# A convolution, matching and cosine-transform kernel: 32-row matmuls widened, image 1 prepared later, norms from row sums, 42 unused matmuls

## The reference

```
x = x + attention(gn(x));   x = x + DCT2(gn(x))        # DCT along H and W, 48 x 48 matrices
attention, for each image:
  embed_w  = prelu(conv1x1(x, Wa));  raw_w = 6x6 patches of it, stride 2        # 576 patches
  match_in = prelu(conv1x1(x, W1));  xp    = 3x3 patches of it                  # 2304 queries
  ref      = prelu(conv1x1(mean over 2x2 of x, W2)); w = 3x3 patches of it      # 576 keys
  wn = w / max(sqrt(sum(w * w)), 1e-4)
  yi = softmax(10 * wn . xp, over the 576 keys)
  y  = transposed convolution of yi with raw_w (stride 2), then a 3x3 convolution Wd, stride 2, + bd, / 6
```

## Time and profile before

| | us |
|---|---|
| median of 3 runs (311.34 to 315.21) | 312.26 |
| the profiled execution, its own time | 313.37 |
| its span | 311.6 |
| TensorE busy in it | 255.3 (82%) |
| VectorE / ScalarE / GpSimd busy | 160.0 / 130.9 / 96.8 |
| chain that ended last, by engine | PE 62%, DVE 21%, issue 8%, ACT 7% |
| mean granted TensorE clock | 0.863 |

### The profile page before, as it was taken

One profiled execution on the slowest core, in us unless ns is written; L12 is line 12 of the kernel. 1 busy time (PEld: TensorE's weight loads), 2 busy tenths in 40 slices (PEclk: granted clock), 3 DMA queues, 4 the chain that ended last, 5 costly groups with the idle time before them and its releaser, 6 DMA issues.

```text
span 311.6 us, 4697 instructions
## 1 busy us (share of the span) xinstructions
PE 255.3 (82%) x1698; PEld 237.3 (76%) x1698; DVE 160.0 (51%) x343; ACT 130.9 (42%) x257; POOL 96.8 (31%) x98
## 2 busy tenths in 40 slices
PE   0458749966599999959989999999989899997085
PEld 0336748955588889949989899999978799996073
DVE  7544163247544363662266446467787664434722
ACT  2053035376346662442256846365646422121020
POOL 6220150077265343144041344339619200000000
PEclk9999999576555895985799999999999999999555
DMA  3430444000003004440000000000300000000321
GB/s 91 108 52 1 70 72 68 1 1 0 3 0 52 2 0 69 68 70 6 2 0 3 0 2 0 2 1 0 78 1 2 0 2 2 0 2 1 63 50 38
DMA packets 11494, 7.67 MB, mean 25 GB/s; under 512 B 8496, under 2 KB 10608, under 8 KB 11344
## 3 DMA queue, kind: packets, MB, share of 16 engines
q1 hardware_dynamic: 11168, 6.94, 12.3%
q10 hardware_dynamic: 304, 0.45, 0.4%
HBM read 2.14 MB, written 1.18 MB: 11 GB/s over the span
## 4 chain that ended last, share of the span: by engine, by line
PE 62%; DVE 21%; issue 8%; ACT 7%; POOL 1%; DVEq 0%; ACTq 0%; POOLq 0%
PE zt L730 21%; PE ps L710 8%; PE yt L745 8%; PE pm L662 6%; PE pm L622 4%; DVE negm L1174 3%; PE pm L684 3%; PE pm L777 3%; DVE yl L1189 3%; PE pd L757 2%; DVE bnst L993 2%; ACT nt L899 2%; DVE v L1212 2%; PE zt L710 2%; PE pm L693 2%
## 5 line engine op out<-in xcount | busy, mean ns | idle before, releaser
L730 PE MATMUL zt<-ident,nt 128*125 128x128 f32 (+1 forms) x720 | 94.8, 284 | 0.0
L730 PEld LDWEIGHTS zt<-ident,nt 128*125 128x125 f32 (+1 forms) x720 | 90.8, 186 | 1.1 <-issue 0.2
L526 POOL TENSOR_TENSOR nt<-nt 128x599 f32<-128x599 f32 (+1 forms) x42 | 56.2, 1338 | 46.9 <-ACT nt L907 39.7
L1189 DVE TENSOR_TENSOR yl<-zt,yh 125x384 fp32r<-125x384 f32 (+1 forms) x60 | 33.4, 556 | 46.6 <-ACT yh L915 15.3
L915 ACT ACTIVATE yh<-zt 125x384 fp32r<-125x384 f32 (+1 forms) x60 | 29.2, 487 | 46.9 <-PE zt L730 46.8
L899 ACT ACTIVATE nt<-ps,negm 128x576 f32<-128x576 f32 x32 | 23.8, 745 | 47.5 <-DVE negm L1174 47.5
L907 ACT ACTIVATE nt<-nt,rps 128x599 f32<-128x599 f32 x36 | 28.7, 798 | 11.8 <-DVE rps L1181 11.5
L516 POOL TENSOR_TENSOR ml<-vim,mh 128x384 fp32r<-128x384 f32 x12 | 12.3, 1029 | 65.3 <-ACT mh L871 65.2
L745 PE MATMUL yt<-yh,kh 125*128 125x384 f32 (+1 forms) x60 | 24.7, 411 | 7.1 <-DVE yl L1189 7.0
L1212 DVE SCALAR_TENSOR_TENSOR v<-pd,v 32x384 f32<-32x384 f32 (+3 forms) x48 | 26.2, 547 | 4.1 <-PE pd L757 2.7
L1174 DVE TENSOR_REDUCE negm<-ps 128x1 f32<-128x576 f32 x32 | 24.1, 753 | 7.6 <-PE ps L710 7.5
(11 more groups left out here) (160 smaller groups left out, 433.1 us busy)
## 6 DMA issues: line engine op xcount, KB each, us to landing
vim<-mimg SPq DMA_DIRECT2D x24, 72.0 KB, 2.5
v<-mimg SPq DMA_DIRECT2D x36, 24.0 KB, 1.9
v<-x SPq DMA_DIRECT2D x2, 288.0 KB, 4.0
vim<-mimg SPq DMA_DIRECT2D x12, 48.0 KB, 2.2
x_copy<-v SPq DMA_DIRECT2D x2, 288.0 KB, 3.1
xr<-x_copy SPq DMA_DIRECT2D x4, 144.0 KB, 2.9
out<-res SPq DMA_DIRECT2D x8, 72.0 KB, 2.2
x<-x SPq DMA_DIRECT2D x6, 72.0 KB, 2.0
```

Source lines behind the costliest of these rows:

```text
L526: pool.tensor_tensor(nt[:, dst, (to + 1) * KP + 1:(to + 1) * KP + 1 + n], nt[:, one, (row1 + 1) * KP + 1:(row1 + 1) * KP + 1 + n], nt[:, o ...
L730: last = nc.tensor.matmul(turned(zt[:, m % 2, :], n, dh, col, JW), keys_at(tile, r + dr, n, shift), ident[:, :], start=at == 0, stop=at == ...
L1189: nc.vector.tensor_tensor(yl[0:n, blk, :].rearrange("p (h j) -> p h j", j=W), turned(zt[:, m % 2, :], n), F(yh[0:n, blk, :]).rearrange("p ...
```

## The change

- The convolutions take no 32-row matmuls. `conv2` and, for image 0, `conv1` use all 128 rows of `x4` in full precision, against weights that are zero outside one quarter (`wb2`, `wb1`, made by one scaling with a mask `smask`). The embedding, and `conv1` of image 1, use a stack of 96 rows `x3`: reduced x, the rest, reduced x again, against stacked weights `wsta`, `wst1`, so that one matmul does the work of three. `x3` is loaded by three DMAs of x per image (`load_copies`).
- The norm adds the squares of three rows on GpSimd first (`sv`), and takes 6 matmuls where it took 18.
- Ahead of the loop the chores have four banks (`bank`), two of them lent by `yt` and `pd`. Keys are scaled and split in halves. The ninth taps of block 0 are loaded from ScalarE's queue.
- The zeroing of the tile edges, of `mr` and of `wr` moves to ScalarE.
- Image 1's x, with one buffer for both images now, is loaded after conv1 of image 0, and its jobs stand in other gaps.
- `warm`: 16, 8, 6 and 12 matmuls of ones with ones into a bank that nobody reads.

The core of the diff:

```
 BEFORE = [
-    ("xs", (0,)), ("mean", (0,)), ("weights", (0,)), ("bias", (0, 1)), ("conv2", (0, 1)), ("low", (0,)),
+    ("xs", (0,)), ("warm", (0,)), ("mean", (0,)), ("weights", (0,)), ("warm", (1,)), ("bias_2", (0,)), ("conv2", (0, 1)), ("bias_1", (0,)),
     ("conv1", (0, 1)), ("squares", (0,)), ("conv1", (2, 3, 4, 5, 6, 7)), ("norm", (0,)),
-    ("inorm", (0, 1)), ("keys", (0,)), ("split", (0, 1)), ("bias", (2,))]
+    ("warm", (2,)), ("inorm", (0, 1)), ("ninth", (0,)), ("xh", (0, 1)), ("keys", (0, 1)), ("split", (0, 1)), ("warm", (3,))]
+
+WARM = (16, 8, 6, 12)
...
 SPREAD = [
-    ("emb", 0, 2, 4, 2), ("ek", 0, 2, 9, 2), ("xs", 1, 1, 13, 1), ("mean", 1, 1, 15, 1), ("weights", 1, 1, 19, 1),
-    ("bias", 1, 3, 22, 1), ("residual", 0, 1, 28, 1), ("conv2", 1, 2, 26, 1), ("low", 1, 1, 27, 1),
-    ("conv1", 1, 8, 29, 1), ("squares", 1, 1, 31, 1), ("norm", 1, 1, 37, 1), ("inorm", 1, 2, 40, 1),
-    ("keys", 1, 1, 42, 1), ("emb", 1, 2, 46, 2), ("ek", 1, 2, 51, 2), ("residual", 1, 1, 60, 1),
+    ("wst", 0, 1, 1, 1), ("xl", 0, 2, 1, 1), ("bias_a", 0, 1, 3, 1), ("emb", 0, 2, 6, 3), ("ek", 0, 2, 12, 2),
+    ("xs", 1, 1, 16, 1), ("mean", 1, 1, 19, 1), ("xh", 1, 2, 20, 1), ("xl", 1, 2, 22, 1), ("weights", 1, 1, 22, 1),
+    ("bias_2", 1, 1, 24, 1), ("wst", 1, 1, 25, 1), ("bias_1", 1, 1, 26, 1), ("conv2", 1, 2, 26, 1), ("bias_a", 1, 1, 28, 1),
+    ("residual", 0, 1, 28, 1), ("conv1", 1, 8, 30, 1), ("squares", 1, 1, 30, 1), ("norm", 1, 1, 35, 1),
+    ("inorm", 1, 2, 39, 1), ("keys", 1, 2, 42, 1), ("emb", 1, 2, 47, 2), ("ek", 1, 2, 52, 2), ("residual", 1, 1, 60, 1),
...
+        def bank(n):
+
+            if n < nbefore:
+                return (pm[:, 0, :], pm[:, 1, :], yt[:, :], pd[:, :])[n % 4]
+            return pm[:, n % 2, :]
...
             def load_x(b, quarters):
                 src = x[b].rearrange("c h w -> c (h w)")
+                if b:
+                    sp.wait_ge(s_mf, misc_no["conv1", b - 1, ROWS - 1] + 1)
...
+            def load_copies(b):
+
+                if b:
+                    sp.wait_ge(s_xl[b - 1], 2)
+                for k in range(3):
+                    sp.dma_start(x3f[C * k:C * (k + 1), :],
+                                 x[b].rearrange("c h w -> c (h w)")).then_inc(s_x3[b], 16)
...
             load_x(0, range(2))
             output_weights()
-            load_x(1, range(4))
+            load_copies(0)
             for b in range(B):
                 sp.dma_start(x1(b), x[b].rearrange("c h w -> c (h w)")).then_inc(s_xin[b], 16)
             sp.dma_start(cosm[:, :], dct).then_inc(s_cos, 16)
             ref_patches(0)
+            load_x(1, range(4))
             match_patches(0)
+            load_copies(1)
             ref_patches(1)
             match_patches(1)
...
-                pool.memset(nt[:, :, 0:KP], 0.0).then_inc(s_tiles, 1)
-                pool.memset(nt[:, :, PT - KP - 2:], 0.0).then_inc(s_tiles, 1)
-                pool.memset(strided(nt[:, 0, :], KP, (PT, NTILES), (KP, HL)), 0.0).then_inc(s_tiles, 1)
...
+                pool.wait_ge(s_sq[b], 2)
+                link(pool.tensor_tensor(sv[:, :], sq[:, 1:1 + L], sq[:, 1 + WL:1 + WL + L], ALU.add))
+                pool.tensor_tensor(sv[:, :], sv[:, :], sq[:, 1 + 2 * WL:1 + 2 * WL + L], ALU.add).then_inc(s_sv[b], 1)
+                pool.wait_ge(s_sv[b], 1)
...
                 n = misc_no[name, b, i]
-                if n >= 2:
-                    wait_emptied(pe, *plan[n - 2])
-                return pm[:, n % 2, :]
+                if n < nbefore:
+                    if n >= 4:
+                        wait_emptied(pe, *plan[n - 4])
+                else:
+                    wait_emptied(pe, *plan[max(n - 2, nbefore - 1)])
+                return bank(n)
...
-                for n, (w, v) in enumerate(((wsh, xh), (wsh, xl), (wsl, xh))):
-                    last = nc.tensor.matmul(o, w[rows, at:at + width], v, start=n == 0, stop=n == 2)
...
-                    last = conv(o[0:96, REFQ * k:REFQ * (k + 1)], q, S_W2, 96, x2h[rows, :], x2l[rows, :])
+                    last = nc.tensor.matmul(o[0:96, REFQ * k:REFQ * (k + 1)], wb2[:, 2 * i + k, :], x2[:, :],
+                                            start=True, stop=True)
...
             def conv1(b, i):
-                if i == 0:
-                    pe.wait_ge(s_wst[b], 1)
-                    pe.wait_ge(s_x4l[b], 1)
+
                 o = misc("conv1", b, i)
-                q, cols = i // 2, slice(HALF * (i % 2), HALF * (i % 2 + 1))
-                rows = slice(C * q, C * (q + 1))
-                conv(o[0:96, 0:HALF], q, S_W1, 96, x4h[rows, cols], x4l[rows, cols]).then_inc(s_mf, 1)
+                if b == 0:
+                    pe.wait_ge(s_wb1, 1)
+                    pe.wait_ge(s_x4[b], 16 * 4)
+                    last = nc.tensor.matmul(o[0:96, 0:HALF], wb1[:, i // 2, :],
+                                            x4[b][:, HALF * (i % 2):HALF * (i % 2 + 1)], start=True, stop=True)
+                else:
+                    pe.wait_ge(s_wst[b], 2)
+                    pe.wait_ge(s_xl[b], i // 4 + 1)
+                    last = nc.tensor.matmul(o[0:96, 0:HALF], wst1[:, :], x3[:, HALF * i:HALF * (i + 1)], start=True,
+                                            stop=True)
+                last.then_inc(s_mf, 1)
...
+                v = x3[:, HALFQ * i:HALFQ * (i + 1)].rearrange("p (i u j v) -> p i u j v", u=2, j=WL, v=2)
+                for n in range(4):
+                    at = C * (3 - n)
+                    last = nc.tensor.matmul(o[:, 0:HALF], wsta[:, at:at + 128], v[:, :, n // 2, :, n % 2],
+                                            start=n == 0, stop=n == 3)
...
-                    for r in range(3):
-                        at = WL * r + 96 * n + 1
-                        last = nc.tensor.matmul(o[0:96, n:n + 1], sq[:, at:at + 96], ones[0:96, 0:1], start=r == 0,
-                                                stop=r == 2)
+                    last = nc.tensor.matmul(o[0:96, n:n + 1], sv[:, 96 * n:96 * (n + 1)], ones[0:96, 0:1], start=True,
...
+            def warm(_, i):
+
+                pe.wait_ge(s_const, 2)
+                for _ in range(WARM[i]):
+                    nc.tensor.matmul(zt[:, 0, 0:128], ones[:, :], ones[:, :], start=True, stop=True)
...
+            def zeros():
+
+                act.wait_ge(s_const, 2)
+
+                def zero(dst, done):
+
+                    shape = list(dst.shape)
+                    one = strided(ones[0:shape[0], :], 0, *[(0, n) for n in shape[1:]])
+                    nc.scalar.activation(dst, one, ACT.Copy, scale=0.0).then_inc(done, 1)
+
+                zero(nt[:, :, 0:KP], s_tiles)
+                zero(nt[:, :, PT - KP - 2:], s_tiles)
+                zero(strided(nt[:, 0, :], KP, (PT, NTILES), (KP, HL)), s_tiles)
+                zero(mr[:, :, :], s_zero)
+                for b in range(B):
+                    zero(wr[b][:, :], s_zero)
...
+            def x3_high(b, i):
+
+                act.wait_ge(s_x3[b], 48)
                 if b:
                     act.wait_ge(s_mf, misc_no["emb", b - 1, 1] + 1)
-                nc.scalar.activation(x4h[:, :], x4[b][:, :], ACT.Copy).then_inc(s_x4h[b], 1)
-                act.wait_ge(s_x2[b], 1)
-                nc.scalar.activation(x2h[:, :], x2[:, :], ACT.Copy, scale=0.25).then_inc(s_x2h[b], 1)
+                cols = slice(HALFQ * i, HALFQ * (i + 1))
+                nc.scalar.activation(x3[:, cols], x3f[:, cols], ACT.Copy).then_inc(s_xh[b], 1)
...
+                for n in range(3):
+                    nc.scalar.dma_start(v2[CR * n:CR * (n + 1), 0:CHUNK],
+                                        mimg[64:64 + CR, at:at + CHUNK]).then_inc(s_mim[0], 16)
...
+            def x3_low(b, i):
+
+                dve.wait_ge(s_xh[b], i + 1)
+                part, cols = slice(C, 2 * C), slice(HALFQ * i, HALFQ * (i + 1))
+                nc.vector.tensor_tensor(x3[part, cols], x3f[part, cols], F(x3[part, cols]),
+                                        ALU.subtract).then_inc(s_xl[b], 1)
...
+                nc.vector.scalar_tensor_tensor(out=wb2[:, :, :], in0=strided(par[:, :], P_W2, (0, 4), (1, 96)), scalar=root,
+                                               in1=strided(smask[:, :, :], 4, (1, 4), (0, 96)), op0=ALU.mult,
+                                               op1=ALU.mult).then_inc(s_wb2[b], 1)
...
+                mid = slice(3 * C, 4 * C)
+                link(nc.vector.tensor_copy(wsta[:, mid], wsf[:, F_WA:F_WA + C]))
+                nc.vector.tensor_tensor(wsta[64:96, mid], wsf[64:96, F_WA:F_WA + C], F(wsta[64:96, mid]),
+                                        ALU.subtract).then_inc(s_wst[b], 1)
...
+            def keys_low(b, i):
+
+                wait_emptied(dve, "inorm", b, i)
+                dve.wait_ge(s_wsc[b], i + 1)
+                dve.wait_ge(s_whi[b], 2 * (i + 1))
+                cols = slice(HALF * i, HALF * (i + 1))
```

(21 more changed lines are left out.)

228 lines of the change are left out of this document (104 added, 124 removed).

## The result

The changed kernel took 277.83 us (median of 277.30 to 278.40), the kernel before beside it 313.05: ratio 0.887, 95% interval 0.881 to 0.893, 11.3% faster. The forecast was 265, in a range of 252 to 285. The profiled execution took 277.30, its span 275.5.

A forecast was written before the change was run, and what follows sets the result against it. The prediction took a chain through all engines to bound the first stage, and TensorE, often at the low clock, the rest. Gains of 14.5, 12.8 and 20.9, together 48.2 us, gave 265 us, in a range of 252 to 285.

The forecast's parts named there:

- First stage: Start to the first score matmul, a chain through all engines: 45.0 us before, 14.5 less, first score at 30.5.
- (a): Start to the mean matmul: zeroing leaves VectorE, 16 unused matmuls stand ahead; mean at 7.3, 1.1 us earlier.
- (b): Mean matmul to the reference image's zeroed edges: fewer scalings and matmuls, 6.2 us instead of 9.4, ready at 13.5.
- (c): Reference edges to match image's edges: four banks, ScalarE sets the pace, 8.8 us instead of 12.3, ready at 22.3.
- (d): Match image's edges to first score: shorter norm, more ScalarE work, GpSimd's split halves; 8.2 us instead of 15.0.
- Fill: First score to group 0's first turned row sums: 45.8 us becomes 33, a gain of 12.8.
- imperfect meshing 1.4: Last term of the 33 us between first score and first turn: 1.4 us for engines' work not fitting together.
- Groups 0 to 2: Three groups after the first turn: clock recovers without 32-row matmuls, fewer passes; 69.9 us becomes 49, a gain of 20.9.
- rival 1: Loop refills: maxima wait behind x parts, row sums behind norm additions, half the loop's gain goes; 282 us, chance 0.18.
- rival 2: The clock does not come back before group 3, so groups 0 to 2 take 68 us; 284 us, chance 0.12.
- rival 3: Low clock lasts behind group 2; from 53 us of it the gain is used up, 393 us with all; chance 0.02.
- Rival 4: More gain: unused matmuls lift first-stage clock (2 us), denser fill (6), groups 1 and 2 lose 5; 252 us, chance 0.12.

The follow-up runs named there:

- first combined version: Changed kernel with x copies behind the first split, fewer unused matmuls, earlier match bias, low parts spread out, conv1 of image 1 at 1.4 steps a tile: 272.5 us.
- experiment 3: Changed kernel with the two low parts of image 1's x on VectorE at steps 28 and 32 instead of 22 and 23: 278.32 us.
- experiment 9: Changed kernel with all of image 1's jobs up to the keys three steps later still: 283.30 us, ratio 0.914.
- experiments 5 and 6: Changed kernel with its 24 stacked matmuls each run three times, over 32 rows (287.24 us) or, as control, over all 96 rows (281.69 us).
- experiments 2 and 7: Changed kernel with two banks before the loop instead of four, 280.76 us; changed kernel with norms by 18 matmuls and no GpSimd additions, 281.23 us.

## Why the prediction was right, and where it was 13 us off

**First stage, 30.5 forecast, 33.15 measured.** (a) The mean came at 7.68 for 7.3: as reckoned, between the ends, the unused matmuls were late (0.19 a pass). Without them the stage is 1.4 us shorter, but the two stages behind it are 1.5 longer: they were neither gain nor loss. (b) 13.5 for 13.5. (c) 22.8 for 22.3, though the bias of conv1 took 1.4 and not 0.4 us. (d) is the term that was mis-sized, 10.3 us for 8.2, and its path was another. ScalarE's first split ended 6.6 us behind the edges, for my 6.4: three issues took 2.13 for 1.3, the rest less. GpSimd's halves took 2.2 more, for my 1.8. What ended last, at 33.00 and 1.3 us behind GpSimd, was VectorE's key parts, for which my sum has no term: beside GpSimd's split a cast of 0.30 took 0.99 and a subtraction of 0.45 took 1.13.

On the price of a full-precision conv1 tile: two such tiles started 0.63 and 0.56 apart at the full clock, and in the first combined version 0.96 apart at the low one:

```profile
12.24 1.17 PE L669 MATMUL yt<-x,wb 128*96 128x288 f32 x2
13.20 1.17 PE L669 MATMUL pd<-x,wb 128*96 128x288 f32 x2
```

By the four passes of the Trainium skill ("FP8 and Floating Point Precision", TensorE Precision Notes) I had estimated 4 x 0.24 = 0.96 at the low level; the trace agrees. My sum stood without that microsecond only because the spacing in the changed kernel was that of the full clock, at 0.6 a tile close to ScalarE's 0.59. The prediction went by the low level, which the rows of before show up to 48 us.

**Fill, 33 forecast, 40.6 measured.** This is the step that failed: "imperfect meshing 1.4" was about 9. Of the terms around it the block ahead of the third maximum (38.47 to 41.88) was 3.4 for my 3.6. Two things have no price in the sum. One is that image 1's mean, scalings and biases pass from VectorE to TensorE and back while both work in order: TensorE waited 7.8 us for them. The other is image 1's pair of low parts, 3.4 us of a VectorE block of 4.9, behind which ScalarE waited 4.25, in part at the same time; I had counted image 0's pair alone. Taking that pair out shortened the fill by 2.7 us (experiment 3), taking more of image 1 out by 4.3 (experiment 9). I blamed the low clock there on 32-row matmuls; it was 0.68 with no 32-row convolution left in the program (0.69 before). From 61.00 to 73.75 it was 0.50, with TensorE busy for 7.1 of 12.75 us. That such waits hold it down is argued from this; experiments 5 and 6 show that rows have a share in the fill as well, 0.63 against 0.72.

**Groups 0 to 2, 49 forecast, 52.6 measured.** 19.8, 14.5 and 18.3 for 18, 14.5 and 16.5. Group 0 had a wait of 2.95 for VectorE's conv1 tile at 82.71. For group 2 my own terms give 29.0 - 8.4 - 3.5 = 17.1 and not 16.5, and the embedding's 8 matmuls, put at 1.1 us, were busy for 2.6: I priced a pass like one of the scores.

The gain of 17.3 us against before has several parts. The largest is group 2's 10.6. Going back to three passes of 32 rows costs 8.2 us there, 3.8 of them by the rows and 4.4 by the passes (26.55, 22.75 and 18.31 us), so the step I gave is shown for group 2: with 32 rows the clock is held down, without them it comes back. Group 1 came out at the forecast 14.5, but not all by the reason I gave: before, its 36 norm passes stood in it, and the clock was 0.50 behind them (118 to 122 us); now the norm stands in group 0, and undoing it costs 2.3 us there and nothing in group 1, while the old places of image 1's jobs cost 3.6 in group 1. For group 0, whose start lies in the stretch from 82.00 to 102.90 that the prediction rested on, the step is not shown: there 32-row conv1 matmuls, each next to long ones, left the clock at 0.92. The before kernel had 0.72; its conv1 also had operands of other row groups, which no run here tried.

**Behind group 2, 0 forecast, -1.7 measured**, 1.3 of it in the long stage and nearly all of that in the first piece of group 3: TensorE was idle there for 1.1 us of 13.16 before, 0.2 of 12.06 after. Before, it waited 1.02 us ahead of 162.89 for VectorE's low part of the turned sums; in the changed kernel that wait is gone, and no run here tells which edit removed it. A change of this stage was one of the signs of being wrong that the prediction named. Of the other two, the third maximum stood behind a block of 3.4 us and not over 5, and the clock was back at 1.00 within about 4 us of group 0's start; it fell once more at the group's end (0.77 from 90.00 to 93.51).

**Rivals.** 277.8 lies nearer to rival 1 (282) than to the forecast. Of the loop's forecast gain of 33.7 us a third, 11.2, did not come, and half of rival 1's mechanism is what happened: maxima behind the x parts waited 3.4 and 3, but TensorE waited for no row sum in groups 0 to 2. Of rival 2 the fill's part came true (0.68), the groups' did not. In rival 3 the 53 us are wrong: with 19 us already lost in the groups, 32 us of the stage at the low level would have used up the rest. Rival 4's first line, unused matmuls that lift the clock, gave nothing.

What each part of the change is worth, by undoing it alone, from the times: stacking to 96 rows 9.4 us (287.2, of which 3.9 are passes and 5.5 rows), image 1's places 5.6, row sums for the norms 3.4, four banks 2.9, the 42 unused matmuls -0.8, within the error. From the ratios, each against the kernel before beside it, the same five are about 11, 8, 4.5, 4.6 and 1, so each is good to some 2 us. By the times they are together some 20 of the 35 us. Of the first stage's 11.9 us experiments 2 and 7 account for 4.2 and 2.9. The moves of the zeroing and of the ninth taps, the halved keys and image 0's convolutions in one full-precision matmul were not tried alone.
